# Front of the kernel with three x slots, angles in pieces and V of the last image early; other first loads in the two attention stages

## What is computed

```python
h = group_norm(x)                                   # 32 groups of 4 channels
q, k, v = h@Wq+bq, (h@Wk+bk)*d**-0.5, h@Wv+bv       # 8 heads, d = 16
qr = q*cos + rotate(q)*sin ; kr = k*cos + rotate(k)*sin
attn = softmax(qr @ kr.T + mask[head])              # mask: (8, 2304, 2304)
x = x + (attn @ v + depthwise5x5(v) + dw_b) @ Wo + bo
t = x + softmax(q1 @ k1.T) @ v1                     # one head of 128, on layer_norm(x)
out = t + layer_norm(experts(layer_norm(t)) + layer_norm(t))
```

## Time and profile before

| | us |
|---|---|
| median of three runs | 3588.86 (3587.58 to 3589.58) |
| the profiled execution | 3589.26, its span 3587.5 |
| front | 0 to 169.5 |
| first attention | 169.5 to 2553.2 |
| second attention and experts | 2553.2 to 3587.5 |

### The profile page before, as it was taken

One profiled execution on the slowest core, in us unless ns is written; L12 is line 12 of the kernel. 1 busy time (PEld: TensorE's weight loads), 2 busy tenths in 40 slices (PEclk: granted clock), 3 DMA queues, 4 the chain that ended last, 5 costly groups with the idle time before them and its releaser, 6 DMA issues. The chain is left out here.

```text
span 3587.5 us, 96344 instructions
## 1 busy us (share of the span) xinstructions
PE 3430.1 (96%) x30684; PEld 2653.5 (74%) x30684; DVE 2622.8 (73%) x6494; ACT 2030.0 (57%) x3660; POOL 1647.8 (46%) x862
## 2 busy tenths in 40 slices
PE   6599999999999999999999999999699999999988
PEld 4377777777777777777777777777477777878867
DVE  6588888888888888888888888888565564644457
ACT  3366666666666666666666666666345454454533
POOL 4565666556565556565566555665300101005112
PEclk9899999999999999999999999999799999999989
DMA  6732232233224224222423422322520110000011
GB/s 198 248 102 96 92 107 96 93 100 102 94 92 132 71 95 133 77 84 99 129 68 100 127 92 69 101 92 67 156 69 29 42 57 12 31 1 1 1 41 43
DMA packets 111227, 308.47 MB, mean 86 GB/s; under 512 B 11512, under 2 KB 72875, under 8 KB 90315
## 3 DMA queue, kind: packets, MB, share of 16 engines
q1 hardware_dynamic: 110507, 306.48, 27.6%
q10 hardware_dynamic: 584, 0.26, 0.0%
HBM read 252.38 MB, written 54.31 MB: 85 GB/s over the span
## 5 line engine op out<-in xcount | busy, mean ns | idle before, releaser
L757 DVE CUSTOM_DVE_ANT_0 c_S<-c_Sps,mask_tiles 128x768 f32<-128x768 f32 x1728 | 1619.3, 956 | 425.8 <-PE c_Sps L808 366.9
L698 ACT ACTIVATE c_PT<-c_Tps 128x512 f32<-128x512 f32 x2592 | 1428.8, 604 | 871.6 <-PE c_Tps L819 809.0
L669 POOL TENSOR_SCALAR c_S<-c_S,c_row_max 128x2304 f32<-128x2304 f32 x576 | 1413.8, 2454 | 946.3 <-DVE c_row_max L768 946.3
L819 PE MATMUL c_Tps<-ident,c_S 128*128 128x128 f32 x10368 | 1399.3, 273 | 4.1 <-ACT c_PT L698 4.1
L819 PEld LDWEIGHTS c_Tps<-ident,c_S 128*128 128x128 f32 x10368 | 1225.9, 140 | 151.5 <-ACT c_PT L698 9.7
L808 PE MATMUL c_Sps<-c_K,c_Q 96*128 (+1 forms) x3456 | 853.5, 328 | 44.4 <-DVEq L738 27.3
L832 PE MATMUL c_Ops<-c_PT,c_V 128*32 128x256 f32 x10368 | 619.1, 382 | 0.8 <-ACT c_PT L698 0.8
L832 PEld LDWEIGHTS c_Ops<-c_PT,c_V 128*32 128x32 f32 x10368 | 307.4, 109 | 243.7 <-issue 50.4
L808 PEld LDWEIGHTS c_Sps<-c_K,c_Q 96*128 96x128 bf16 x3456 | 314.8, 98 | 203.5 <-issue 144.4
L1359 DVE TENSOR_SCALAR_CACHE_REDUCE l_S<-l_Sps 128x384 f32<-128x384 f32 x432 | 240.4, 557 | 293.9 <-PE l_Sps L1182 267.2
L1095 ACT ACTIVATE ln2T<-l_Tps 128x384 f32<-128x384 f32 x432 | 196.6, 491 | 404.6 <-PE l_Tps L1203 404.6
(11 more groups left out here) (204 smaller groups left out, 1662.2 us busy)
## 6 DMA issues: line engine op xcount, KB each, us to landing
mask_tiles<-in_mask SPq DMA_DIRECT2D x144, 1152.0 KB, 7.7
numerators<-c_O SPq DMA_DIRECT2D x288, 64.0 KB
mask_tiles<-numerators SPq DMA_DIRECT2D x7, 2304.0 KB, 8.6
q_parts<-f_parts SPq DMA_DIRECT2D x12, 576.0 KB, 7.6
k_parts<-f_parts SPq DMA_DIRECT2D x12, 576.0 KB
c_Q<-q_parts SPq DMA_DIRECT2D x71, 96.0 KB
c_vpad<-v_padded SPq DMA_DIRECT2D x8, 756.0 KB, 15.0
c_K<-k_parts SPq DMA_DIRECT2D x7, 864.0 KB, 8.7
```

The lines of the kernel that those rows point to most:

```text
L669: pool.tensor_scalar(S[:, slot, :], S[:, slot, :], -1.0, row_max[:, slot:slot + 1], ALU.mult, ALU.add).then_inc(shifted, 1)
L698: act.activation(dst, src, ACT.Exp, scale=-1.0).then_inc(exp_done, 1)
L757: dve.tensor_tensor_reduce(out=S[:, r % ROW_SLOTS, cols(CH, c)].rearrange("p (k n) -> p k n", k=2), in0=Sps[:, n % S_SLOTS, :, 0:GW], in1= ...
L819: last = pe.transpose(Tps[:, g % T_SLOTS, cols(P, k)], S[:, (2 * b + t) % ROW_SLOTS, cols(P, kt)], ident[:, :])
```

## The change

The front has three x slots instead of two, so x of images 1 and 2 are loaded at the start and x of image 3 after image 0. Weights, rows and taps are issued by ScalarE. Cosine and sine come as 128 rows, laid out so in memory, in three pieces each with a semaphore of its own. Two mask tiles are loaded, between x of image 1 and x of image 2; the other two come in the first attention. The statistics of the next image are taken two groups a step in steps 0 to 2, its normalisation is in step 4. The early loads of head 0 are made for images 0 and 1, at the end of images 1 and 2; those of image 2 move to the first attention. In the last image all twelve V groups are made in steps 0 to 2, and the padded image is stored ahead of the q parts. In the first attention, SyncE loads image 2, the padded half, image 3, a mask pair and q, in that order; TensorE waits for images 2 and 3 at rows 4 and 6. The denominators of the second attention are loaded at the end of the first, and both halves are summed before the biases are copied.

Core of the diff (left out: slot numbers `b % 2` to `b % X_SLOTS`, semaphore counts for the new order of V, arguments):

```diff
-weights_in, angles_in, mask_in = sem("weights_in"), sem("angles_in"), sem("mask_in")
-x_first, x_in = sem("x_first"), [sem("x0_in"), sem("x1_in")]
+weights_in, mask_in = sem("weights_in"), sem("mask_in")
+angles_in = [sem(f"angles{c}_in") for c in range(NCH)]
+x_first, x_in = sem("x_first"), [sem(f"x{b}_in") for b in range(B)]
...
-def place_of(g, image):
+def place_of(b, g, image):
+    if b == B - 1:
+        return g // 2 * 4 + 2 * image + g % 2
     return NG + g + (NG + g >= MEANS) if image else g
+def use_of(b, g, image):
+    place = place_of(b, g, image)
+    return VPS_USES * b + place - (b < B - 1 and place > MEANS)
+def v_work(b, step):
+    if b == B - 1:
+        return [(image, 2 * step + g) for image in (False, True) for g in range(2)] if step < NCH else []
+    return [(step >= NCH, 2 * (step % NCH) + g) for g in range(2)]
...
     def store_v(b):
-        sp.wait_ge(vps_taken, VPS_USES * b + NG)
+        sp.wait_ge(vps_taken, VPS_USES * b + (NG if b < B - 1 else VPS_USES - 2))
...
     load_x(0)
-    for i, w in enumerate((a["Wq"], None, a["Wk"], None, a["Wv"])):
-        if w is not None:
-            sp.dma_start(weights[:, i, :], w).then_inc(weights_in, 16)
-    for i, v in enumerate((a["bq"], None, a["bk"], None, a["bv"], a["dw_b"])):
-        if v is not None:
-            sp.dma_start(rows[:, i, :], v.rearrange("(a n) -> a n", a=1)).then_inc(weights_in, 16)
-    sp.dma_start(taps_row[:, :], a["dw_w"].rearrange("a b o c -> (a b o) c")).then_inc(weights_in, 16)
-    sp.dma_start(cosT[:, :], s["cosT"].unsqueeze(0).to_broadcast([HEADS, D, N])).then_inc(angles_in, 16)
-    sp.dma_start(sinT[:, :], s["sinT"].unsqueeze(0).to_broadcast([HEADS, D, N])).then_inc(angles_in, 16)
+    for c in range(NCH):
+        sp.dma_start(cosT[:, cols(CH, c)], s["cosT"][:, cols(CH, c)]).then_inc(angles_in[c], 16)
+        sp.dma_start(sinT[:, cols(CH, c)], s["sinT"][:, cols(CH, c)]).then_inc(angles_in[c], 16)
     load_x(1)
+    for it in range(2):
+        sp.dma_start(mask[:, it, :], s["mask"][it]).then_inc(mask_in, 16)
+    load_x(2)
...
         store_v(b)
-        if b:
+        if b == B - 1:
+            store_vpad(b)
+        store_parts(b, 0)
+        if b < B - 1:
+            store_vpad(b)
+        if b + X_SLOTS < B:
+            sp.wait_ge(mm_ready, 2 * STEPS * (b + 1))
+            load_x(b + X_SLOTS)
+        if b in (1, 2):
             load_early(b - 1)
-        sp.dma_start(mask[:, b, :], s["mask"][b]).then_inc(mask_in, 16)
-        store_parts(b, 0)
-        store_vpad(b)
-        if b + 2 < B:
-            sp.wait_ge(mm_ready, 2 * STEPS * (b + 1))
-            load_x(b + 2)
     store_parts(B - 1, 1)
-    sp.wait_ge(early_in, 16 * EARLY_LOADS * (B - 1))
+    sp.wait_ge(early_in, 16 * EARLY_LOADS * 2)
...
+    for i, w in enumerate((a["Wq"], None, a["Wk"], None, a["Wv"])):
+        if w is not None:
+            act.dma_start(weights[:, i, :], w).then_inc(weights_in, 16)
+    for i, v in enumerate((a["bq"], None, a["bk"], None, a["bv"], a["dw_b"])):
+        if v is not None:
+            act.dma_start(rows[:, i, :], v.rearrange("(a n) -> a n", a=1)).then_inc(weights_in, 16)
+    act.dma_start(taps_row[:, :], a["dw_w"].rearrange("a b o c -> (a b o) c")).then_inc(weights_in, 16)
...
             u = STEPS * b + step
-            for g in range(2):
-                if step < NCH:
-                    take_v(b, 2 * step + g)
-                else:
-                    take_v_image(b, 2 * (step - NCH) + g)
-                if g == 0 and u:
+            for k, (image, g) in enumerate(v_work(b, step)):
+                if k == 1 and u:
                     first_part(u - 1)
+                (take_v_image if image else take_v)(b, g)
+            if not v_work(b, step):
+                first_part(u - 1)
...
                 second_part(u - 2)
-            if step == STEPS - 2 and b + 1 < B:
+            if step == 3 and b + 1 < B:
...
                 pe.wait_ge(norm_step, 3)
-            for g in range(2):
-                if step < NCH:
-                    v_tokens(b, 2 * step + g)
-                else:
-                    v_image(b, 2 * (step - NCH) + g)
+            for image, g in v_work(b, step):
+                (v_image if image else v_tokens)(b, g)
...
         b, m, c = at(u)
+        if u < NCH:
+            dve.wait_ge(angles_in[c], 32)
...
     dve.tensor_tensor(conv_bias[:, :], biases[:, 4:5], biases[:, 5:6], ALU.add).then_inc(small_taken, 1)
-    dve.wait_ge(angles_in, 32)
...
                 variance(b + 1)
-            if b + 1 < B and step == STEPS - 1:
+            if b + 1 < B and step == 4:
...
             with_sin(u)
-            if b + 1 < B and step in (1, 2):
-                statistics(b + 1, range(NG // 2 * (step - 1), NG // 2 * step))
+            if b + 1 < B and step < 3:
+                statistics(b + 1, range(2 * step, 2 * step + 2))
...
 k_in, v_in, q_in, mask_in = sem("k_in"), sem("v_in"), sem("q_in"), sem("mask_in")
+image_in = [None, None, sem("image2_in"), sem("image3_in")]
...
-    sp.sem_inc(mask_in, 32 * 2)
+    sp.sem_inc(mask_in, 32)
+    sp.sem_inc(k_in, 48)
+    sp.sem_inc(q_in, 48)
+    sp.sem_inc(v_in, 16)
+    load_first_head(sp, s, K, Q, V_next, 2, [image_in[2]] * 3)
     load_half(0)
-    load_first_head(sp, s, K, Q, V_next, B - 1, (k_in, q_in, v_in))
-    sp.wait_ge(q_in, 48)
+    load_first_head(sp, s, K, Q, V_next, 3, [image_in[3]] * 3)
+    load_mask(1)
...
     sp.wait_ge(o_stored, 16 * STORES * (PAIRS + 2))
+    sp.dma_start(first_den[:, :, :], s["den_load"][0]).then_inc(den_in, 16)
...
         images = cols(B // 2 * TILES, half)
-        if not first or half:
+        if not first:
             act.wait_ge(v_in, 16 * (h + 1))
+        elif half:
+            act.wait_ge(image_in[2], 16 * EARLY_LOADS)
+            act.wait_ge(image_in[3], 16 * EARLY_LOADS)
...
-        if c == 0 and r == (ROWS - 2 if first else 0):
+        if r == 0 and c == 0 and not first:
...
             pe.wait_ge(k_in, 48 * (ip // HEAD_PAIRS + 1))
+        if first and c == 0 and r in (4, 6):
+            pe.wait_ge(image_in[r // 2], 16 * EARLY_LOADS)
...
 PT = ln2T[:, 3, :].rearrange("p (t q) -> p t q", t=TILES)
-den = sb("den", [P, 4, SEG])
+den = first_den
...
-    sp.dma_start(den[:, :, :], s["den_load"][0]).then_inc(den_in, 16)
...
     def sum_first(half):
-        dve.wait_ge(first_sum, 2 * half + 1)
+        dve.wait_ge(first_sum, half + 1)
...
     def finish_first(half):
-        dve.wait_ge(first_sum, 2 * half + 2)
+        dve.wait_ge(first_sum, half + 3)
...
     invert(0)
+    sum_first_pairs(1)
     sum_first(0)
+    sum_first(1)
...
         last.then_inc(small_taken, 1)
-    sum_first_pairs(1)
-    sum_first(1)
...
 first_num = ln2[:, :, :].rearrange("p t c -> p (t c)").rearrange("p (f j n) -> p f j n", f=2, j=4)
+first_den = ctx.enter_context(nc.sbuf_tensor("first_den", [P, 4, N // D], F32))
+den_in = ctx.enter_context(nc.semaphore("den_in"))
...
     "xT": lambda x: x.reshape(B, N, C).transpose(0, 2, 1),
-    "sinT": lambda x: x.reshape(N, D).T,
-    "cosT": lambda x: x.reshape(N, D).T,
+    "sinT": lambda x: np.tile(x.reshape(N, D).T, (HEADS, 1)),
+    "cosT": lambda x: np.tile(x.reshape(N, D).T, (HEADS, 1)),
```

More of the change, by code:

```diff
@@ L342, in bank_free @@
                 elif place > 1 or b:
-                    pe.wait_ge(vps_taken, VPS_USES * b + place - 1 - (place - 2 > MEANS))
+                    pe.wait_ge(vps_taken, VPS_USES * b + place - 1 - (place - 2 > MEANS and b + 1 < B))
             def group_means(b):
@@ L373, in project @@
                 for k in range(2):
-                    last = pe.matmul(mm[:, use % MM_SLOTS, k, 0:GW], weights[:, 2 * m + r, :], XT[:, b % 2, cols(GW, 2 * c + k)],
+                    last = pe.matmul(mm[:, use % MM_SLOTS, k, 0:GW], weights[:, 2 * m + r, :], XT[:, b % X_SLOTS, cols(GW, 2 * c + k)],
                                      start=True, stop=True)
```

45 lines of the change are left out of this document (22 added, 23 removed).

## The result

The changed kernel takes 3567.6 us in the median (3566.66 to 3570.54), against 3588.9 before: ratio 0.9944, 95% interval 0.9930 to 0.9957. The forecast was 3560.0, the range 3550 to 3571. The profiled execution took 3568.93, its span 3567.1, 20.4 us under that of before.

The account below looks back on a forecast made before the run. TensorE bounds the long middle stage; in the front no engine does, but waits for loads, VectorE work and k stores. 28.9 us saved less 1.2 plus 1.0 is 28.7, from 3589.3 to 3560.6, by the median 3560; range 3550 to 3571.

Parts of the forecast that it names:

- part 1: Head: angles in three 128-row pieces, weights on ScalarE's queue; first angle product at 17.1 us instead of 31.16, second at 21.9.
- part 2: Front: x of image 1 behind the angles and three x slots remove 6.4 us of x waits.
- late-x rival: Front, step 0: loads at 225 GB/s leave VectorE and TensorE standing 4 us, time 3564; chance 0.05.
- part 3: Front, images 0 to 2: respread statistics and normalisation give 26.2 us each, plus 0.9 k-part wait in images 1 and 2.
- "quicker" rival: Front, images: VectorE's excess fully hidden behind TensorE and no wait for k parts, time 3553; chance 0.08.
- port rival: Front: the moved normalisation waits one GpSimd instruction of 1.64 us in each of three images, time 3565; chance 0.05.
- part 4: Front, image 3: V in three steps costs 4.7 us by itself; VectorE ends at 133.3, 16.5 us saved.
- part 5: Tail: last k part lands 5.0 us after issue, middle stage opens at 140.6 instead of 169.5, 28.9 us saved so far.
- the stores pace the front: Front: stores ready in bunches, engine share 0.72, end at 144, 5 us later, time 3565; chance 0.12.
- part 6: Start of the first attention: later loads of image 3's V and the padded half cost 1.2 us, bounds 0.4 and 3.
- The rival with 0.42 us per pair in the loop: First attention's loop: transfers settle at another phase; from 0.42 us per pair the gain is gone, at 0.6 3603; chance 0.03.
- part 7: Second attention: denominators loaded early, inverses start about 1.5 us sooner, 1.0 us saved, bounds -0.4 and 3.

## Why the prediction was right, and where it was off

**Head (part 1): right, for the reason given.** The products were put at 17.1 and 21.9 and came at 17.18 and 21.54. The full rate, taken as 331 GB/s, was 414. (The text counts three V groups before the second product; the 1.5 us it uses are those of two, which is what ran.) The run with the old form shows what the form alone is worth at the end, 13.8 us by the medians. That this is near the 14.0 by which the first product came earlier is chance: there it cost 2.4 us at the first product and the rest by a late x.

**x (part 2): right.** VectorE waits 5.2 us for x in all, the start; none later. The old form brought the late-x rival to life, at 227 GB/s for its 225: 8.0 us of waiting for x of image 1, where 4 were foreseen.

**Images 0 to 2 (part 3): forecast a little too slow in images 0 and 1, too quick in image 2.** 24.8 and 24.5 us against 27.1 for each: VectorE's excess in step 2 and step 4 is hidden behind TensorE, which is busy throughout, as the "quicker" rival had it. Image 2 took 28.6. The start of image 3 was put at 98.4 and is at 95.1, in spite of a wait for stored k parts that was sized at 0.9 us per image and measured 2.1 in image 1 and 5.2 in image 2. The direction of that wait was seen and its size was not, since I took the k stores' landing time for a matter of load. "ScalarE waiting over 2 us for stored parts" was one of the prediction's own signs of being wrong, and it came; it pointed at these stores. The port rival did not come: the moved normalisation lasts 1.5 to 1.6 us in every image (up to 1.9 before).

**V early (part 4): price near, worth wrong.** Priced at 4.7 us in image 3; it costs 6.0 there by the run without it. ScalarE's wait of 3.9 us for the padded image, which is in no term, is gone in that run. "It pays in the tail" is the sentence that failed: 0.7 us.

**Tail (part 5): the term that was mis-sized.** From VectorE's end to the next stage I had 7.3 us (1.2 to issue, 5.0 to land, 1.1 to open); it is 14.2 (3.7, 9.5 and 1.0). The 5.0 was argued from the load on the engines, 265 GB/s wanted of 268 moved, within the landing of 3.9 to 8.8 us. That landing is not one of a k store. Those 3.9 to 8.8 us are the landings of q stores, whose outermost dimension is 128; for a k store the profile of the kernel before shows none:

```profile
q_parts<-f_parts SPq DMA_DIRECT2D x12, 576.0 KB, 7.6
k_parts<-f_parts SPq DMA_DIRECT2D x12, 576.0 KB
```

What it does show of the k stores is SyncE's wait of 12.4 us for the last of them. And it was no matter of load: a k store is slow with the engines to itself, and quick in its other form. The page DMA: Bandwidth & Descriptors of the Trainium skill (Rules for kernel authors) says that an outermost dimension of eight confines a transfer to at most eight engines; I weighed that rule for the loads that the change rewrites, and did not hold it against the stores that it leaves alone. By it the share in a stretch with k stores alone is 0.5 at most, and 0.41 to 0.50 was measured. 28.9 us were forecast for the front and 24.2 came: 2.2 more than forecast up to VectorE's end, 6.9 less in the tail.

The rival "the stores pace the front" had the last store landed at 144, and it landed at 144.3. Its number came, its reason did not: it took the sum of all stores at a share of 0.72, but in the other form the last store landed 2.8 us behind its piece, and not 13.2.

**First attention (part 6): +1.2 forecast, +2.3 in the trace.** The place was right (ScalarE's copy of image 3's V): exponentials 1.5 us later, and 0.6 more at the end from the early load, where I had charged nothing to this stage. The rival with 0.42 us per pair in the loop did not come: TensorE's busy time is 2355.6 against 2356.0.

**Second attention (part 7): 1.0 forecast, nothing found.** The inverses leave 2.1 us earlier (+4.8 instead of +6.9) and are read back at +9.1 instead of +9.3. SyncE waits 4.0 us for the store to land instead of 2.0. In between, the numerators and the weights are loading. Two stretches of the kernel after, up to the store's issue and from there to its landing:

```profile
2532.00:2536.00 4.00, 0.00 (x0) 0.00 (x0) 3.92 (x7) 0.00 (x0) 4.00 (x6) 0.50 1.07 212
2536.00:2540.40 4.40, 0.00 (x0) 0.00 (x0) 4.40 (x5) 0.00 (x0) 4.40 (x3) 0.50 0.66 238
```

The engines are full up to the store's issue, and two thirds busy while it is under way. That it waits behind those loads is the reading that fits both orders; it was not tested by itself. The step that failed is "what passes through is the 1.5 less 0.4": I followed VectorE's and TensorE's chain and not the queue that the store goes through. On GpSimd's side, the page SBUF — State Buffer (Trainium skill, Who interferes with whom) has it that a VectorE operation with two inputs in SBUF contends with a GpSimd operation that reads SBUF. The trace agrees: eight operations of 0.32 us took 4.7 with one of them held to 2.64, and 9.6 with several, and nothing depended on them.

In sum: -24.2 (front), +2.3 (first attention), +1.3 (second, by the clock of that execution) and +0.2 behind it make the 20.4 us between the two spans. The forecast had 28.7. The 8.3 us between are 6.9 in the tail, less 2.2 up to it, 1.1 in the first attention, 2.3 in the second (the 1.0 not gained, and 1.3 by its clock) and 0.2 behind; the medians put the miss at 7.6. Some luck is in it: up to VectorE's end the front was quicker than forecast, which hid part of the tail.

## What to carry to other kernels

When a rule on the form of a transfer explains one slow load, go through every other transfer of that kernel with it, stores too, before a landing time is put down to load; a share of the DMA engines near one half while something waits for them was the mark here, though the angle loads in eight copies ran at half the rate with a full share. A slow transfer is paid for by what stands behind it in the queue and by each engine that waits for its buffer, so moving its neighbours shifts the waits, as the early loads did, and changing its form removed them here. And a difference of 1 us in one stretch of one trace is no finding until a second trace has the same granted clock there.

## What the runs showed of the hardware

- The same 576 KB store, with 128 rows outermost, is issued in 0.34 us and lands in 2.8 (median of the last three; 3.7 over all twelve), at 288 GB/s in the tail. With 8 outermost the last three took 1.4 to 3.1 us to issue and paced the tail at 167 to 197 GB/s, with a share of 0.41 to 0.50.
- Loads handed out as eight copies, and what stood behind them in the queue, ran at 227 GB/s with the share at 1.00, where 128-row loads moved 414 at 1.04. A full share is thus no proof of a full rate.
- The rest of the program behind the first q copy lasted 980.5 to 981.2 us in five traces and 982.4 to 983.4 in nine, without regard to any edit here; this two-valued scatter of 2 us (the kernel after has one trace in each group) is as large as most of the smaller effects above.
- GpSimd's operation on an 8x16 tile took 0.32 us, and up to 2.64 beside VectorE's sums with both inputs in SBUF; eight of them took anything from 4.7 to 9.6 us.
- The same TensorE work costs more at a lower granted clock: some 24 matmuls took 3.3 us at 0.95 and 5.0 at 0.50, and the stretch to the first q copy took 51.1 us at 0.93 and 54.7 at 0.74 (its part from 40 us on). Which of the levels a build got there no edit explains.
